# A DLRM tower in blocks of 256 samples with 11 resident tables, instead of blocks of 512 with 9 tables loaded again in each

## The chip, the cores and the metric

One core of one Trainium2 chip. The metric is the device time of one launch in microseconds (us), as the median of several runs.

## What is computed

For each of 2048 samples the kernel fetches one row of 128 floats from each of 26 tables, stacks them behind the sample's dense row (27 features), takes all 351 inner products between two different features, and puts the result through three layers:

```
e = stack([tbl_f[ids[:, f]] for f in range(26)], axis=1)
combined = concatenate([dense[:, None, :], e], axis=1)          # 2048 x 27 x 128
inter = einsum('bfd,bgd->bfg', combined, combined)[:, iu, ju]   # 351 pairs
h = concatenate([dense, inter, dense], axis=1)                  # 2048 x 607
h = maximum(h @ W_top1 + b_top1, 0)                             # 512
h = maximum(h @ W_top2 + b_top2, 0)                             # 256
y = h @ W_top3
```

Twelve tables have 1000 rows, the others 1250, 12500 or 125000. All is in float32. Where the fast float32 matmul (fp32r) is used, an operand is split into a high and a low part, so one product costs two or three matmuls.

## The kernel before

The batch runs in 4 blocks of 512 samples (4 tiles of 128). Three blocks are passes of a loop (`Fori`), the last is written out after it. Inside a block every engine follows two lists made by hand, `BODY` and `TAIL`; in the same lists the tables of the next block are looked up ("ahead").

- **Gathers.** GpSimd (POOL) fetches 17 tables: one indirect DMA (L396) for each table and tile, 128 rows each, 272 in all. TensorE (PE) transposes the rows (`embed`, L416) in groups of 4 features into a PSUM bank, and ScalarE (ACT) copies the bank into `emb` (L535), whose layout is [dimension, sample, feature].
- **Lookups.** 9 tables of 1000 rows are looked up by matmul. For each block and table SyncE (SP) loads the whole table (L331) and the ids, broadcast to 128 partitions (L335). ACT takes the high part (L543), VectorE (DVE) the low part (L640). For each of 8 chunks of 125 rows DVE makes a one-hot of 125x512 (L650), and PE multiplies it with the high and the low part (L436, L438). ACT copies the result into one column of `emb` (L549, L558).
- **Gram.** For each sample PE multiplies `emb[:, s, 1:27]` with `emb[:, s, 0:26]` (L454), four samples side by side in the array; 64 samples fill one bank (128 matmul records, as a float32 matmul leaves two). DVE copies the bank (L663) and transposes 32x32 blocks (L670). ACT, and DVE for the last tile, copy the upper triangle row by row into `pairs` (L565, L677).
- **Layers.** PE transposes `pairs` (`z`, L467), ACT and DVE make high and low parts (L574, L687); layer 1 is 192 and layer 2 is 96 matmuls of 512 columns over all blocks (L485 to L488, L498 to L501). ACT and DVE split the hidden layer (L586, L588, L699). ACT sends y out (L604).

Of the kernel before, what the change touches and what calls it, by code (L numbers as in the profile page):

```python
# [8 lines left out]
FEATURES = TABLES + 1  # L29
# [3 lines left out]
LOOKUPS = 9  # L33
LOOKED_UP = [t for t in range(TABLES) if VOCAB[t] == 1000][:LOOKUPS]
GATHERED = [t for t in range(TABLES) if t not in LOOKED_UP]

ORDER = [0] + [t + 1 for t in GATHERED] + [t + 1 for t in LOOKED_UP]


def pair_rows():  # L40

    rows = []
    for r in range(FEATURES):
        for s in range(r + 1, FEATURES):
            a, b = sorted((ORDER[r], ORDER[s]))
            rows.append(DIM + a * FEATURES - a * (a + 1) // 2 + (b - a - 1))
    return rows


def dlrm_tower(nc, dense, ids_gathered, ids_looked_up, tables, w1_dense, w1_pairs, b1, w2, b2, w3,  # L50
               out):
    fp32, fp32r = mybir.dt.float32, mybir.dt.float32r
    i32, u32 = mybir.dt.int32, mybir.dt.uint32
# [5 lines left out]
    NG = len(GATHERED)  # L59
    ROWED = NG + 1  # L60

    EMBED = [list(range(f, min(f + 4, ROWED))) for f in range(0, ROWED, 4)]
    bank_of = {f: e for e, features in enumerate(EMBED) for f in features}
    CHUNKS = 8
    TROWS = 1000 // CHUNKS
    SIDE = FEATURES - 1
    HALF = 16
    GRAMS = TILE // 4 // HALF * TILES
    KCH = [128, 128, PAIRS - 256, DIM]
    N1, N2 = HIDDEN1 // 128, HIDDEN2 // 128  # L70
    ONE_HOTS = 9
    assert LOOKUPS * CHUNKS % ONE_HOTS == 0

    EARLY = 2
    lookups = [("lookup", i, h) for i in range(LOOKUPS) for h in range(2)]  # L80
    early, halves = lookups[:2 * EARLY], lookups[2 * EARLY:]
    embeds = [("embed", t, e) for t in range(TILES - 2) for e in range(len(EMBED))]

    PARTS = ((3,), (0,), (1, 2))
    LAST = len(PARTS) - 1
    own = [[("layer1", 0, 0)], [("layer1", 1, 0), ("z", 0, 0), ("z", 1, 0), ("z", 2, 0)],
           [("z", 0, 1), ("z", 1, 1)], [("z", 2, 1)],
           [("layer1", 0, 1)], [("layer1", 1, 1)], [("layer1", 0, 2)], [("layer1", 1, 2)],
           [("layer1", 2, p) for p in range(3)], [("layer1", 3, p) for p in range(3)], "E",
           [("layer2", 0)], [("layer2", 1)], "E", [("layer3",)], "E", "E", "E", "E", "E", "E"]  # L90
    TAIL = [("place", i) for i in range(EARLY)] + [("pair", 1)] + halves[:1]
    spaces = own.count("E")
    for k, steps in enumerate(own):
        if steps == "E":
            n = len(embeds) // spaces
            spaces, steps, embeds = spaces - 1, embeds[:n], embeds[n:]
        TAIL += steps

        upto = -(-(k + 1) * len(halves) // len(own))
        if "E" in own[k + 1:k + 2]:  # L100
            upto += upto % 2
        TAIL += [s for s in halves[:upto] if s not in TAIL]
    assert len(TAIL) == len(set(TAIL))
    tile2, tile3 = ([("embed", t, e) for e in range(len(EMBED))] for t in (2, 3))
    BODY = [("gram", 0), ("gram", 1), ("gram", 2), *tile2, ("gram", 3), ("gram", 4),
            *early, *tile3[:-1], ("dense",), ("gram", 5, 0), tile3[-1], ("gram", 5, 1),
            ("split", EARLY + 1), ("pair", 0), ("gram", 6), ("gram", 7)]

# [6 lines left out]
        [("layer2", n) for n in range(N2)] + [("layer3",), ("none",)]  # L115
    assert len(MLP_USES) % 2 == 0
    assert len(EMB_USES) % 3 == 0 and len(MIX_USES) % 3 == 0

    PAIR_TILES = [slice(0, TILES - 1), slice(TILES - 1, TILES)]
# [648 lines left out]
```

## Time and profile before

| | |
|---|---|
| median of 3 runs | 432.58 us (428.92 to 434.95) |
| profiled execution, span from first to last instruction | 432.4 us |
| PE, PEld (weight loads), POOL, DVE, ACT busy | 330.4, 266.8, 308.9, 239.1, 179.4 us |
| granted TensorE clock, mean | 0.881 of 2.4 GHz |

The profiled execution has no other time of its own than its span; it stands 0.2 us under the median. Busy time of an engine is the time in which an instruction of it runs. In the timeline a line is one instruction or several alike; its columns are the start, the length, the engine, the source line and the operation, and in brackets the idle time of the engine before it with what ended it ("issue": nothing that the profile shows). In a line of a group the numbers after the bar are busy time, mean ns of one, and the idle time before.

### The profile page before, as it was taken

What the parts mean: (1) busy time and instruction counts of PE and PEld (TensorE: products, weight loads), DVE (VectorE), ACT (ScalarE), POOL (GpSimd) and SP (SyncE); (2) the same over time, 40 slices, a digit from 0 to 9 for tenths busy, and PEclk for the clock granted to TensorE, in tenths of its full rate; (3) what the DMA queues carried; (4) which work ended last, traced back from release to release, by engine and by line L of the source; (5) the groups of instructions that cost most, each with busy time, mean ns of one, the idle gap of its engine ahead of it and who ended that gap; (6) DMA issues with size and microseconds to landing.
All of it is one profiled execution on the core that took longest, in us unless ns stands there. A gap on an engine that the chain in (4) does not pass through costs nothing.

```text
span 432.4 us, 13310 instructions
## 1 busy us (share of the span) xinstructions
PE 330.4 (76%) x5360; PEld 266.8 (62%) x5360; DVE 239.1 (55%) x471; ACT 179.4 (41%) x363; POOL 308.9 (71%) x280
## 2 busy tenths in 40 slices
PE   0785719677699998286879999376969999867596
PEld 0563517466578876275668877264758887656475
DVE  2776625397569563266768664075666758023531
ACT  2144223720746546220546545420564546323442
POOL 6887878887778877777778878777777877772000
PEclk9899977888979999659969999666879999986699
DMA  5467853435435345426444543526354442221000
GB/s 155 153 177 191 239 167 109 128 92 151 115 110 149 118 122 117 133 52 167 119 130 114 158 116 106 141 55 169 77 172 100 142 123 71 55 57 28 5 0 0
DMA packets 24707, 49.51 MB, mean 115 GB/s; under 512 B 8010, under 2 KB 10586, under 8 KB 24653
## 3 DMA queue, kind: packets, MB, share of 16 engines
q1 hardware_dynamic: 15916, 30.83, 22.4%
q0 software_dynamic: 8704, 17.84, 17.5%
q8 instruction: 47, 0.77, 0.7%
q14 instruction: 8, 0.06, 0.0%
q10 hardware_dynamic: 32, 0.01, 0.0%
HBM read 48.65 MB, written 0.01 MB: 113 GB/s over the span
## 4 chain that ended last, share of the span: by engine, by line
PE 65%; issue 15%; DMA 10%; ACT 5%; DVE 3%; SPq 0%; ACTq 0%; DVEq 0%
PE mix_ps L454 12%; PE emb_ps L436 12%; PE emb_ps L438 11%; PE emb_ps L416 6%; DMA lookup_ids<-ids_looked_up 5%; DMA table<-table 5%; PE mlp_ps L485 4%; PE mlp_ps L488 4%; PE mlp_ps L486 4%; PE mlp_ps L436 3%; PE mlp_ps L438 3%; DVE one_hot L650 2%; ACT emb L535 2%; PE mlp_ps L498 2%; PE mlp_ps L501 2%
## 5 line engine op out<-in xcount | busy, mean ns | idle before, releaser
L396 POOL DMA_INDIRECT rows<-table,gather_ids x272 | 307.9, 1132 | 83.6 <-issue 81.7
L650 DVE TENSOR_SCALAR one_hot<-lookup_ids,row_number 125x512 fp32r<-125x512 int32 x288 | 124.8, 490 | 43.6 <-DMA lookup_ids<-ids_looked_up 17.6
L436 PE MATMUL emb_ps<-one_hot,table_h 125*128 125x512 f32 x224 | 94.2, 421 | 19.1 <-DVE table_l L640 18.7
L454 PE MATMUL mix_ps<-emb 128*26 128x26 f32 x4096 | 57.7, 202 | 54.3 <-issue 51.5
L438 PE MATMUL emb_ps<-one_hot,table_l 125*128 125x512 f32 x224 | 91.9, 410 | 0.0
L454 PEld LDWEIGHTS mix_ps<-emb 128*26 128x26 f32 x4096 | 49.5, 115 | 63.6 <-issue 61.7
L543 ACT ACTIVATE table_h<-table 125x1024 fp32r<-125x1024 f32 x36 | 38.0, 1060 | 88.9 <-DMA table<-table 52.4
L535 ACT ACTIVATE emb<-emb_ps 128x512 f32<-128x512 f32 (+1 forms) x80 | 46.9, 651 | 56.5 <-PE emb_ps L416 53.2
L663 DVE COPY gram<-mix_ps 128x416 f32<-128x416 f32 x32 | 27.8, 874 | 74.3 <-PE mix_ps L454 74.1
L436 PEld LDWEIGHTS emb_ps<-one_hot,table_h 125*128 125x128 f32 x224 | 44.6, 199 | 31.7 <-ACT emb L535 12.1
L549 ACT ACTIVATE emb<-emb_ps 128x512 f32<-128x512 f32 x28 | 34.0, 1215 | 50.2 <-PE emb_ps L438 50.1
L640 DVE TENSOR_TENSOR table_l<-table,table_h 125x1024 fp32r<-125x1024 f32 x36 | 43.6, 1212 | 13.6 <-ACT table_h L543 13.6
L438 PEld LDWEIGHTS emb_ps<-one_hot,table_l 125*128 125x128 f32 x224 | 44.7, 200 | 9.2
L436 PE MATMUL mlp_ps<-one_hot,table_h 125*128 125x512 f32 x64 | 31.0, 484 | 20.2 <-DVE one_hot L650 17.5
L416 PE MATMUL emb_ps<-ident,rows 128*128 128x128 f32 x272 | 42.7, 302 | 1.9 <-ACT emb L549 1.7
L416 PEld LDWEIGHTS emb_ps<-ident,rows 128*128 128x128 f32 x272 | 36.0, 158 | 6.9 <-ACT emb L549 1.9
L436 PEld LDWEIGHTS mlp_ps<-one_hot,table_h 125*128 125x128 f32 x64 | 15.0, 235 | 26.0 <-issue 15.0
L438 PE MATMUL mlp_ps<-one_hot,table_l 125*128 125x512 f32 x64 | 29.8, 466 | 0.0
L565 ACT ACTIVATE pairs<-turned 128x24 f32<-128x24 f32 (+33 forms) x148 | 19.0, 219 | 11.7 <-DVE turned L670 11.7
L699 DVE TENSOR_TENSOR h1l<-h_full,h1h 128x512 fp32r<-128x512 f32 x16 | 11.2, 700 | 22.0 <-ACT h1h L588 22.0
L586 ACT ACTIVATE h_full<-mlp_ps,b_sb 128x512 f32<-128x512 f32 x16 | 11.0, 689 | 20.7 <-PE mlp_ps L488 20.6
L485 PE MATMUL mlp_ps<-zh,w1h 128*128 128x512 f32 (+1 forms) x48 | 19.1, 398 | 0.5 <-ACT zh L574 0.5
(50 smaller groups left out, 278.4 us busy)
## 6 DMA issues: line engine op xcount, KB each, us to landing
table<-table SPq DMA_DIRECT2D x36, 500.0 KB
lookup_ids<-ids_looked_up SPq DMA_DIRECT2D x36, 256.0 KB, 5.4
rows<-table,gather_ids POOLq DMA_INDIRECT x272, 3.9
dense_rows<-dense SPq DMA_DIRECT2D x4, 256.0 KB, 4.1
gram<-w_pairs SPq DMA_DIRECT2D x2, 256.0 KB
gram<-w_dense SPq DMA_DIRECT2D x2, 256.0 KB
h_full<-w SPq DMA_DIRECT2D x1, 512.0 KB
gather_ids<-ids_gathered SPq DMA_DIRECT2D x16, 8.5 KB, 10.2
```

The source lines that it names most:

```text
L396: pool.indirect_dma_start(out=rows[:, t, g, :], out_offset=None, in_=tables[GATHERED[g]], in_offset=bass.IndirectOffsetOnAxis(ap=gather_id ...
L416: last = pe.transpose(bank[:, 128 * k:128 * k + 128], src, ident[:, :])
L436: pe.matmul(bank[:, :], table_h[0:TROWS, i % 2, cols], hot, start=(c == 0), stop=False)
L438: last = pe.matmul(bank[:, :], table_l[0:TROWS, i % 2, cols], hot, start=False, stop=(c == CHUNKS - 1))
L454: last = pe.matmul(bank[32 * j:32 * j + SIDE, SIDE * q:SIDE * q + SIDE], emb[:, s, 1:FEATURES], emb[:, s, 0:SIDE], start=True, stop=True)
L485: pe.matmul(mlp_bank(("layer1", n))[:, :], w1h[0:k, c, cols], high, start=(c == 3), stop=False)
L535: act.activation(emb[:, t * TILE:(t + 1) * TILE, EMBED[e][0]:EMBED[e][0] + k], emb_bank(("embed", t, e))[:, 0:128 * k].rearrange("p (k s) ...
L543: act.activation(table_h[0:TROWS, i % 2, :], table[0:TROWS, i % 2, :], ACT.Copy) \
L549: act.activation(emb[:, :, ROWED + i], emb_bank(("lookup", i, 1))[:, :], ACT.Copy) \
L640: dve.tensor_tensor(table_l[0:TROWS, i % 2, :], table[0:TROWS, i % 2, :], table_h[0:TROWS, i % 2, :].bitcast(fp32), ALU.subtract) \
L650: dve.tensor_scalar(one_hot[0:TROWS, hot_slot(i, c), :], lookup_ids[0:TROWS, i % 2, :], row_number[0:TROWS, c:c + 1], None, ALU.is_equal) \
L663: dve.tensor_copy(gram[:, :, HALF * n:HALF * n + HALF].rearrange("p r q -> p q r"), mix_bank(("gram", n))[:, 0:SIDE * HALF].rearrange("p ( ...
```

## The change

The kernel is written anew around one list, `STEPS`: each step gets a time in units of a block (`at(time, ...)`), the list is sorted by it, and each engine runs its part of the list, written out without a loop.

- 8 blocks of 256 samples, that is 16 tiles of 128.
- 11 tables are loaded once. Their high and low parts stay in SBUF (`table_hl`). `raw`, where they land, has 6 slots and lies on the half of `emb` that block 1 uses first. In block 0 only 6 of them are looked up, from block 1 on all 11: 83 lookups. The first lookup of block 1 waits for all 11 low parts.
- Tiles 0 and 1 gather 20 tables, the other 14 tiles gather 15: 250 gathers. The rows lie in a ring of 7 groups; a gather waits until PE has transposed the group 7 before. The dense row is the last feature of a tile's last group.
- A one-hot is 128x256 from 16-bit ids; the ring holds 8. A chunk is 128 rows (tables are padded to 1024). Two tables share a PSUM bank and are copied together.
- A gram bank (64 samples) is filled in one run (`BURSTS = 1`). ACT copies it instead of DVE. A tile's triangle is copied by 10 ACT instructions, in bands of 5 rows.
- Layer matmuls have 256 columns; there are 384 and 192 of them. ACT writes the hidden layer's full value back into its PSUM bank, and DVE subtracts from there.
- The build takes `dynamic_dma_scratch_size=4096`.

The core of the diff:

```diff
-    TILE, TILES = 128, 4
-    BLOCK = TILE * TILES
+    TILE = 128
+    TILES = BATCH // TILE
     BLOCKS = BATCH // BLOCK
+    GROUP = [grouped(list(range(FIRST_LOOKUPS if t < BLOCK // TILE else LOOKUPS, FEATURES))) for t in range(TILES)]
+    ROW_SLOTS = 7
+    HALF, BURSTS = 16, 1
+    HOTS = 8
+    RAW, LIDS = 6, 4
+    LOOKS = [(b, i) for b in range(BLOCKS) for i in range(LOOKUPS if b else FIRST_LOOKUPS)]
+    def look_time(k, h):
+        b, i = LOOKS[k]
+        return b - 1 + (i + h / 2) / (LOOKUPS if b else FIRST_LOOKUPS) + (0.02 if b else 0.0)
+    def embed_time(t, e):
+        return (t / 2 - 0.7 if t >= 3 else (-0.2, 0.25, 0.56)[t]) + 0.06 * e * 4 / len(GROUP[t])
+    for i in range(LOOKUPS):
+        at(-1.6 + 0.1 * i if i >= RAW else -2.0 + i / 100, "load", i)
+        at((-1.5, -1.3)[i] if i < 2 else -1.1 + 0.1 * i, "split", i)
+    for k in range(len(LOOKS)):
+        at(look_time(k - LIDS, 1) + 0.002 if k >= LIDS else -1.995 + k / 100, "lids", k)
+        for h in range(2):
+            at(look_time(k - 1, h) + 0.001 if k >= 1 else -1.4 + h / 50, "hots", k, h)
+            at(look_time(k, h), "look", k, h)
...
+                at(t / 2 + 0.05 + 0.24 * (n % 2) + 0.06 * h + (0.07 if t == 1 else 0.0), "gram", n, h)
+        at(t / 2 + 0.54, "pairs", t)
...
+        for c in range(2):
+            at(u + 1.06 + 0.02 * c, "z", u, c)
+        for n in range(N1):
+            at(u + 1.13 + 0.09 * n, "l1", u, n)
+        for n in range(N2):
+            at(u + 1.54 + 0.09 * n, "l2", u, n)
+        at(u + 1.74, "l3", u)
...
             def hots(k, h):
...
+                    wait(dve, hot_used, n - HOTS + 1)
+                    dve.tensor_scalar(hot[:, n % HOTS, :], lids[:, k % LIDS, :],
+                                      row_number[:, c:c + 1], None, ALU.is_equal).then_inc(hot_ready, 1)
...
             def look(k, h):
...
+                    if k < FIRST_LOOKUPS:
+                        pe.wait_ge(table_low, k + 1)
+                    elif k == FIRST_LOOKUPS:
+                        pe.wait_ge(table_low, LOOKUPS)
...
+                for e, group in enumerate(GROUP[t]):
+                    use = GROUP_NO[t, e]
+                    wait(pool, embeds_done, use - ROW_SLOTS + 1)
...
-    nc = bacc.Bacc("TRN2", target_bir_lowering=False, num_devices=1)
+    nc = bacc.Bacc("TRN2", target_bir_lowering=False, num_devices=1, dynamic_dma_scratch_size=4096)
```

## Rows read from the trace of the kernel before

**Rows 1.** The page: busy tenths, and the granted clock, in 40 slices of 10.8 us.

```profile
PE   0785719677699998286879999376969999867596
...
PEclk9899977888979999659969999666879999986699
```

**Rows 2.** Groups of instructions by line: the gathers.

```profile
L396 POOL DMA_INDIRECT rows<-table,gather_ids x272 | 307.9, 1132 | 83.6 <-issue 81.7
```

**Rows 3.** Timeline of all engines: the last gather, and the last row transposes.

```profile
392.28 0.94 POOL L396 DMA_INDIRECT rows<-table,gather_ids  x1 [0.30 <-issue]
...
397.76 0.44 PE L416 MATMUL emb_ps<-ident,rows 128*128 128x128 f32 x2
```

**Rows 4.** All gathers of line 396: first and last start, and the time to landing.

```profile
L396 POOL DMA_INDIRECT rows<-table,gather_ids x272: 940/947/3814, 2.7 to 392.3; - x136
...
DMA to landing us min/median/max: 2.4/3.9/8.0
```

**Rows 5.** Timeline of PE: gram runs, at the low clock, then at the high one.

```profile
179.76 2.03 PE L454 MATMUL mix_ps<-emb 128*26 128x26 f32 x127 [2.48 <-issue]
183.79 1.97 PE L454 MATMUL mix_ps<-emb 128*26 128x26 f32 x127 [2.00 <-issue]
...
399.08 1.28 PE L454 MATMUL mix_ps<-emb 128*26 128x26 f32 x128 [0.42 <-issue]
402.90 1.28 PE L454 MATMUL mix_ps<-emb 128*26 128x26 f32 x128 [2.55 <-issue]
```

**Rows 6.** Who waited for whom: PE in the gram.

```profile
PE mix_ps L454 <- issue: 51.5, 26, 3.9
```

**Rows 7.** Timeline of PE: 512-column steps, low clock, after a wait, 72 at the high clock.

```profile
12.84 0.63 PE L436 MATMUL mlp_ps<-one_hot,table_h 125*128 125x512 f32 x1
13.27 0.63 PE L438 MATMUL mlp_ps<-one_hot,table_l 125*128 125x512 f32 x1
...
17.34 0.50 PE L436 MATMUL mlp_ps<-one_hot,table_h 125*128 125x512 f32 x1 [1.91 <-DVE one_hot L650]
...
129.02 0.40 PE L436 MATMUL emb_ps<-one_hot,table_h 125*128 125x512 f32 x1
...
145.80 0.39 PE L436 MATMUL emb_ps<-one_hot,table_h 125*128 125x512 f32 x1
```

**Rows 8.** Timeline of PE: row transposes, at the high clock and at the low one.

```profile
170.44 1.04 PE L416 MATMUL emb_ps<-ident,rows 128*128 128x128 f32 x8
189.45 3.56 PE L416 MATMUL emb_ps<-ident,rows 128*128 128x128 f32 x17
```

**Rows 9.** Timeline of DVE and POOL in two bursts of DVE.

```profile
16.80 4.84 DVE L650 TENSOR_SCALAR one_hot<-lookup_ids,row_number 125x512 fp32r<-125x512 int32 x12
...
18.10 1.28 POOL L396 DMA_INDIRECT rows<-table,gather_ids  x1 [0.30 <-issue]
19.68 2.07 POOL L396 DMA_INDIRECT rows<-table,gather_ids  x1 [0.30 <-issue]
22.06 0.94 POOL L396 DMA_INDIRECT rows<-table,gather_ids  x1 [0.30 <-issue]
```

**Rows 10.** Groups by line, of DVE and ACT.

```profile
L650 DVE TENSOR_SCALAR one_hot<-lookup_ids,row_number 125x512 fp32r<-125x512 int32 x288 | 124.8, 490 | 43.6 <-DMA lookup_ids<-ids_looked_up 17.6
...
L543 ACT ACTIVATE table_h<-table 125x1024 fp32r<-125x1024 f32 x36 | 38.0, 1060 | 88.9 <-DMA table<-table 52.4
...
L549 ACT ACTIVATE emb<-emb_ps 128x512 f32<-128x512 f32 x28 | 34.0, 1215 | 50.2 <-PE emb_ps L438 50.1
L640 DVE TENSOR_TENSOR table_l<-table,table_h 125x1024 fp32r<-125x1024 f32 x36 | 43.6, 1212 | 13.6 <-ACT table_h L543 13.6
```

**Rows 11.** Windows of one block each: busy time by engine, clock, DMA share.

```profile
172.00:272.00 100.00, 80.79 (x1346) 66.08 (x1346) 58.17 (x116) 44.55 (x93) 78.59 (x71) 0.88 0.45 124
```

**Rows 12.** Windows of 4 us at the start, the same columns, GB/s last.

```profile
7.00:11.00 4.00, 0.00 (x0) 0.00 (x0) 0.92 (x1) 1.06 (x1) 3.08 (x4) 1.00 0.76 221
44.00:48.00 4.00, 4.00 (x20) 3.20 (x19) 1.58 (x5) 0.83 (x1) 3.08 (x4) 1.00 1.05 306
```

More of the change, by code:

```diff
@@ L40, in pair_rows @@
 def pair_rows():
     rows = []
[L43 to L46, printed above, removed]
-    return rows
-def dlrm_tower(nc, dense, ids_gathered, ids_looked_up, tables, w1_dense, w1_pairs, b1, w2, b2, w3,
-               out):
+    for r, s in pair_list():
+        a, b = sorted((ORDER[r], ORDER[s + 1]))
+        rows.append(DIM + a * FEATURES - a * (a + 1) // 2 + (b - a - 1))
@@ L104, in dlrm_tower @@
[L104 to L107, printed above, removed]
-    EMB_USES = [s for s in TAIL + BODY if s[0] == "embed" or (s in halves and s[2] == 1)]
-    MIX_USES = [("gram", n) for n in range(GRAMS)] + [("z", 0), ("z", 1), ("z", 2)] + [("none",)]
@@ new lines, in dlrm_tower, with pair_of_looks @@
+    for j in range(6):
+        at(0.05 + 0.13 * j, "weights", j)
+    for u in range(BLOCKS):
+        late = u == BLOCKS - 1
+        for c in range(2):
[5 more added lines that the diff above has]
+        at(u + 1.74, "l3", u)
+    STEPS = [step for _, _, step in sorted(timed)]
+    def pair_of_looks(k):
+        first = k - LOOKS[k][1] % 2
+        return first, min(first + 1, k - LOOKS[k][1] + len([1 for b, _ in LOOKS if b == LOOKS[k][0]]) - 1)
@@ L378, in _ @@
+            sp.dma_start(gather_ids[:, 0, :], ids_gathered[:, 0, :]).then_inc(first_ids_in, 16)
+            run({"load": load, "lids": load_lids, "drow": drow, "weights": weights})
         @block.gpsimd
@@ L440, in lookup @@
-                    last.then_inc(hot_used, 1)
-            def grams(b, n, part=None):
-                if n % 2 == 0:
-                    need = [u for u in EMB_USES if u[0] == "lookup" or u[1] == n // 2]
-                    pe.wait_ge(emb_copied, emb_no(b, need[-1]) + 1)
-                if part != 1:
-                    pe.wait_ge(*mix_before(b, ("gram", n)))
-                bank = mix_bank(("gram", n))
-                for q in (range(HALF) if part is None else range(HALF)[part * HALF // 2:][:HALF // 2]):
+                    pe.matmul(bank, table_hl[:, i, 0, cols], hot[:, n % HOTS, :], start=(c == 0), stop=False)
@@ new lines, in look, with embed @@
+                    pe.matmul(bank, table_hl[:, i, 1, cols], hot[:, n % HOTS, :],
+                              start=False, stop=(c == CHUNKS - 1)).then_inc(hot_used, 1)
+            def embed(t, e):
+                use, n = ("embed", t, e), GROUP_NO[t, e]
+                pe.wait_ge(rows_in[n % ROW_SLOTS], rows_landed(n))
+                if e == len(GROUP[t]) - 1:
+                    pe.wait_ge(dense_in[t % 2], 16 * (t // 2 + 1))
+                wait_emb_bank(pe, use)
+                for q in range(len(GROUP[t][e])):
+                    last = pe.transpose(emb_bank(use)[:, 128 * q:128 * q + 128], rows[:, n % ROW_SLOTS, q, :], ident[:, :])
+                last.then_inc(embeds_done, 1)
@@ new lines, in gram @@
+            def gram(n, h):
+                t, side = n // 2, n % 2
+                bank = mix_ps[n % 2]
+                if h == 0:
+                    if side == 0:
+                        b = t // 2
+                        pe.wait_ge(emb_placed, max(
+                            [placed["look", pair_of_looks(k)[1], 1] for k in range(len(LOOKS)) if LOOKS[k][0] == b] +
+                            [placed["embed", t, e] for e in range(len(GROUP[t]))]))
+                    wait(pe, gram_out, n - 1)
+                for q in range(h * HALF // BURSTS, (h + 1) * HALF // BURSTS):
```

836 lines of the change are left out of this document (369 added, 467 removed).

## The prediction

> **What bounds the kernel now.** I read the page first, then the groups by line, the waits, and the timeline of each engine. PE is busy nearly throughout, and in every block there are some slices at five or six tenths in which the clock falls as well [rows 1]. But busy shares don't name the bound. POOL issues 272 gathers; behind each it idles 0.30 us, put down to "issue", so it waits for nobody [rows 2], and it goes on from 2.7 to 393.2 us [rows 3, 4]. That is 390.5 / 272 = 1.436 us a gather. The last rows land some 4 us later, and PE's last two row transposes start at 397.76, as soon as they can [rows 3, 4]. From there to the end (432.4) it is 34.7 us of layers. So the gathers set the end, with that tail behind them.
>
> PE is bound just as tightly. Its steps at the high clock (2.4 GHz): a 512-column matmul 0.232 us (190 steps between lines such as 133.95 and 134.19), at the low clock (1.2 GHz) 0.427 [rows 7]; a row transpose (1.04 - 0.3) / 7 = 0.106 us, at the low clock 0.204 [rows 8]; a gram bank 1.28 us, at the low clock 2.03 [rows 5]. Before: 864 x 0.232 + 336 transposes x 0.106 + 32 banks x 1.28 = 200 + 36 + 41 = 277 us at the high clock, some 2 us of layer 3 with it 279. The rest up to 432 is 51.5 us of idle "issue" in the gram [rows 6], the start, the tail, and the low clock, which holds (1 - 0.881) x 2 = 24% of the time. After each 128 records of gram PE stands still for 2 to 2.5 us, so that a bank takes about 4 us whatever the clock [rows 5]. 128 matmuls and their 128 weight loads are 256 instructions, 16 KB.
>
> The page of the Trainium skill on Runtime: NRT & Kernel Launch (Instruction fetch mechanics) says that instructions come in blocks of 16 KiB, 256 of them, and that a taken branch breaks the prefetch. The gaps of 2.0 us after 127 or 128 records [rows 5] agree with the block size. By that rule a run of 64 samples amid slower work finds its block there.
>
> **The change, POOL.** 250 gathers instead of 272. Undisturbed one takes 0.94 + 0.30 = 1.25 us [rows 3, 4]: 250 x 1.25 = 312.5. What lies above that is DVE: during 12 one-hots in a row (4.84 us) gathers took 1.28 and 2.07 us, behind it 0.94 again [rows 9]. All stalls before: 307.9 - 272 x 0.944 = 51 us [rows 2, 4], on 288 one-hots 0.18 us each [rows 10]. After there are 83 x 8 = 664 one-hots, but of 256 columns: one of 512 steps every 4.84 / 12 = 0.40 us [rows 9]; taken as 0.13 fixed + 0.27 for the columns, half of it is 0.26, and all are 664 x 0.26 = 173 us against 115. Bounds: nothing (0), and 664 x 0.18 = 120 us if each one costs as much as now. Between them: a gather waits for the rest of the DVE instruction that runs, which goes with count x length squared: 664 x 0.26^2 / (288 x 0.40^2) = 0.97, so 50 us; with burst time (1.85 against 1.25 us a gather in the burst [rows 9]) it is a third of 173 = 58. I take 55, near both. POOL ends at 2.7 + 312.5 + 55 = 370, the last rows land at 374.
>
> The Trainium skill, SBUF — State Buffer (Who interferes with whom), has it that a DVE instruction in a two-port mode locks GpSimd out for its whole length. [rows 9] agree. By a strict lock with no gap between one-hots the stall would go with their whole time, 173 us instead of 55; the two gathers that got through within the 4.84 us speak against that.
>
> The ring of 7 groups lets POOL be 23 gathers ahead at the start. Gather 24 needs the first embed group, which PE does behind its fifth lookup, at about 30 us; POOL is there at 2.7 + 23 x 1.47 = 37. It costs nothing; if lookups start 10 us late it costs 3. The smaller descriptor memory: issue to landing is 3.9 us [rows 4], so 3 to 4 gathers are under way. I take 0 for it, and its upper end is a rival.
>
> **PE.** Lookups are 83 x 16 = 1328 matmuls of 256 columns, layers 576. No row shows 256 columns. Below: 256 / 2.4 = 0.107. Above: the first matmul after a wait took 0.50 instead of 0.39 to 0.40 us [rows 7], so a weight load that nothing hides costs 0.11, and 0.107 + 0.11 = 0.217. The nearest row is the transpose, which loads 128 columns of weights each and still steps by 0.106 [rows 8]; so the load hides behind 0.107. 512 columns step by 0.232, 0.019 over 512 / 2.4; kept whole it gives 0.126, halved 0.116. I take 0.126. Sum: 1904 x 0.126 = 240, (266 + 48) transposes x 0.106 = 33, 32 banks x 1.28 = 41, layer 3 1: 315 us against 279. PE thus gets 36 us more work; what it should get back is the 51.5 us in the gram, since a gram bank is now followed by 20 to 50 slower instructions at a time. I leave 10 us of gaps in the whole (a third of the banks run out of instructions for 1 us).
>
> **The start.** Before, only two tables were under way, and one was loaded each 6 to 9 us. Now six go out at once: 3.0 MB at 221 GB/s [rows 12] is 14 us, and the memory queues have given 306. DVE then is the slowest: up to the first lookup of block 1 it has 52 one-hots x 0.26 and 11 low parts x 1.21 [rows 10] = 27 us behind about 11, so 38 us. PE would be quick enough, but tile 3's rows, gather 70, come at 2.7 + 70 x 1.47 (the pace of the DVE-laden start) + 3.9 = 109.5. PE waits for them, since embed stands in its list before the lookups of block 2. Behind them PE has 1632 matmuls x 0.126 = 206, 240 transposes 25, 28 banks 36, 1: 268 us, plus 10 of gaps, plus 16 idle in the tail: 404 at the high clock throughout. With a tenth of the time at the low clock it is 268 / 0.95 = 282, so 418. POOL's path and PE's path are again nearly even.
>
> **The tail.** Behind the last embed stand four gram banks (5), 12 transposes (1), 144 layer matmuls x 0.126 (18), layer 3 (0.3): 25 us. The chain of the last bank waits for ACT's copy (1.0), DVE's transposes (1.05), the triangle (10 x 0.22), high and low parts before layer 1 (1.4), before layer 2 (1.4), and the output (3), and block 6 has two such waits of 1.5: with the hand-overs 16 us. So 41, with 0.5 for the embed and 1.5 for the low clock 43.
>
> **Sum.** 2.7 + 312.5 + 55 + 3.9 + 43 = 417.1 us, against 432.4 of the profiled span, which is the median of the runs shown (432.58) within 0.2. All other edits lie beside this: 25 splits of tables fewer on ACT and DVE (25 x 1.06 and 25 x 1.21 us [rows 10]); the gram copies on ACT (32 x 1.0); ACT comes to some 205 us and DVE to 235 of 417. If that cover went, each late step of ACT would cost PE its 1 us, some 14 times. DMA moves about 29 MB instead of 49.5 and is at 45% of its time now [rows 11].
>
> **Rivals.**
> 1. Slower: one-hots cost POOL by their count, 0.18 us each, 120 us. For it: the first burst [rows 9], where gathers took up to 2.07 us. Against: shorter instructions leave sooner. 2.7 + 312.5 + 120 + 47 = 482 us. It decides from (432.4 - 2.7 - 312.5 - 47) / 664 = 0.106 us a one-hot.
> 2. The 256-column step isn't half: each 10 ns over 0.126 costs 16 us on PE's path; from 0.141 the kernel is no faster, at 0.217 it takes 404 + 1632 x 0.091 = 553. Against: the transposes [rows 8].
> 3. PE's clock and small waits: at the low clock for 24% of the time as now, 268 / 0.88 = 305, so 441 us. For it: PE waits for rows in every tile, as POOL is even with it. Against: the slices at the low clock now stand at the gram's gaps [rows 1, 5], which go.
> 4. Better: short one-hots let the gathers through (25 us of stalls), a step of 0.116, 5 us of gaps: POOL's path 2.7 + 312.5 + 25 + 47 = 387, PE's 404 - 16 - 5 + 7 for the clock = 390, and some waits, 395 us.
> 5. The change doesn't do what it says: the smaller descriptor memory lets one gather go at a time, 250 x 3.9 = 975 us. Against: nothing in the trace shows that it is full.
>
> **How the numbers follow.** The forecast has 38%, rival 4 22%, rival 3 17%, rival 1 and what lies between it and the forecast 13%, rival 2 7%, rival 5 3%. Predicted: 417 us. The range, 392 to 450, takes in rival 4, rival 3 and the lower part of rival 1. A measurement of this kernel tells 2% (424 to 441 is no change). Faster: rival 4 and the forecast whole, 60%; same: rival 3 and the mild cases of 1 and 2, 22%; slower: the rest of 1, 2, 3 and 5, 18%.
>
> **What would show it.** Gathers that end near 370 with a mean of about 1.47 us from start to start; the 256-column step at 0.126; gram banks of 1.3 us without a gap of 2 us behind most of them; PE waiting for rows up to about 110 us; a tail of 43 us behind the last landing; a mean clock over 0.92. The prediction is wrong if POOL ends before 340 or after 400, if the step is over 0.14, or if PE never waits for rows and yet ends late.

## The result, and the profile after

| | before | after |
|---|---|---|
| median (runs) | 433.68 us (428.92 to 434.95, 4) | 397.9 us (397.15 to 398.95, 4) |
| span of the profiled execution | 432.4 us | 395.9 us |
| mean granted clock | 0.881 | 0.966 |

The ratio is 0.920, 95% interval 0.914 to 0.926: 8% faster, where 3.6% (417 us) was forecast. It stands inside the range, near the time of rival 4.

The page of the changed kernel: busy time by engine, and busy tenths with the granted clock in 40 slices of 9.9 us.

```profile
PE 344.4 (87%) x6378; PEld 323.1 (82%) x6378; DVE 261.1 (66%) x765; ACT 183.2 (46%) x443; POOL 239.5 (61%) x258
...
PE   1777499458999999999999999999999899998556
...
POOL 6777777777777777777777676757674752000000
PEclk9989889988999999999999999999999989999969
```

The dips of PE and of the clock in every block [rows 1] are gone: from slice 11 to 36 PE is at 80% or more and the clock nearly full. Groups by line, gathers, one-hots and gram, against [rows 2, 10] (after the bar: busy us, mean ns, idle before):

```profile
L340 POOL DMA_INDIRECT rows<-table,gather_ids x250 | 238.6, 954 | 91.5 <-issue 73.5
L571 DVE TENSOR_SCALAR hot<-lids,row_number 128x256 fp32r<-128x256 int16 x664 | 206.1, 377 | 27.7 <-PE emb_ps L368 24.9
...
L394 PE MATMUL mix_ps<-emb 128*26 128x26 f32 x4096 | 53.0, 193 | 6.9 <-issue 3.4
```

All gathers of the changed kernel (min/median/max ns, first and last start), with POOL's idle time, against [rows 4]:

```profile
L340 POOL DMA_INDIRECT rows<-table,gather_ids x250: 940/944/1802, 2.7 to 330.7; - x125
its engine sat idle before it (us, times) until:
  issue: 73.5, 241
  PE emb_ps L378: 17.0, 8
```

A gather takes 954 ns on average instead of 1132: next to nothing holds it up. POOL even waits 17.0 us for PE (the ring is full), and is through at 331.6, 64 us ahead of the end. PE's waits (us in total, times, longest):

```profile
PE emb_ps L367 <- DVE hot L571: 19.6, 9, 8.0
PE emb_ps L378 <- DMA rows<-table,gather_ids: 10.6, 5, 3.4
PE mix_ps L394 <- issue: 3.4, 2, 1.9
```

The 51.5 us of "issue" in the gram [rows 6] have come down to 3.4. This list leaves out idle times of less than 0.15 us, and there are such pauses: most gram banks take about 1.8 us or more. One of the middle, and one of those later on (timeline of PE):

```profile
207.52 1.82 PE L394 MATMUL mix_ps<-emb 128*26 128x26 f32 x128
302.67 1.27 PE L394 MATMUL mix_ps<-emb 128*26 128x26 f32 x128
```

From the start of the first matmul of a bank to the start of what follows it, 23 of the first 25 banks take 1.7 us or more, and the six from 325 us to 368 us take 1.2 to 1.3. In the bank at 207.52 two matmuls start 0.22 and 0.27 us behind the one before them, which the bank at 302.67 doesn't have; the weight loads in it wait 0.18 us for "issue". What these pauses are is not shown.

The chain of work that ended last, by engine, and the timeline where it passes from POOL to PE:

```profile
PE 68%; POOL 16%; issue 8%; ACT 3%; DVE 2%; DMA 1%
```

```profile
87.01 0.95 POOL L340 DMA_INDIRECT rows<-table,gather_ids  x1 [0.30 <-issue]
...
90.49 1.11 PE L378 MATMUL emb_ps<-ident,rows 128*128 128x128 f32 x4 [3.39 <-DMA rows<-table,gather_ids]
...
94.35 0.60 PE L378 MATMUL emb_ps<-ident,rows 128*128 128x128 f32 x4
```

Those at 90.49 are the third of tile 3's four groups. Its last gather, the 70th, starts at 90.76, and its last group is transposed at 94.35 without a wait. By the chain the gathers set the pace up to 90.5 us, from there PE alone. Three windows, split at 90.5 and behind the last row transposes (us, then busy and count of PE, PEld, DVE, ACT, POOL, the clock, the DMA share, GB/s):

```profile
0.00:90.50 90.50, 57.92 (x835) 51.63 (x835) 63.95 (x162) 37.13 (x61) 67.99 (x77) 0.92 0.52 155
90.50:354.20 263.70, 257.97 (x4859) 245.59 (x4860) 189.33 (x588) 127.03 (x320) 171.54 (x181) 0.99 0.28 66
354.20:395.90 41.70, 28.46 (x688) 25.85 (x685) 7.81 (x15) 19.04 (x63) 0.00 (x0) 0.92 0.01 2
```

In the middle PE is busy 98% of the time at 0.99 of full clock.

### The profile page after: what moved, and what is told of

The parts are those of the page before. It is cut to its first block, busy times and chain, and to the rows that moved or that the text cites. A ratio compares the mean times of both kernels' runs of the same rounds, so it can differ in the third digit from the quotient of the medians.

```text
span 395.9 us, 14710 instructions
## 1 busy us (share of the span) xinstructions
PE 344.4 (87%) x6378; PEld 323.1 (82%) x6378; DVE 261.1 (66%) x765; ACT 183.2 (46%) x443; POOL 239.5 (61%) x258
## 4 chain that ended last, share of the span: by engine, by line
PE 68%; POOL 16%; issue 8%; ACT 3%; DVE 2%; DMA 1%
PE emb_ps L367 17%; POOL rows L340 16%; PE emb_ps L368 16%; PE mix_ps L394 11%; PE emb_ps L378 6%; PE mlp_ps L425 4%; PE mlp_ps L427 4%; PE mlp_ps L426 4%; PE mlp_ps L436 2%; PE mlp_ps L438 2%; PE mlp_ps L437 2%; ACT gram_sb L491 1%; PE mlp_ps L447 1%; DVE hot L571 1%; PE mlp_ps L407 1%
## 5 line engine op out<-in xcount | busy, mean ns | idle before, releaser
L340 POOL DMA_INDIRECT rows<-table,gather_ids x250 | 238.6, 954 | 91.5 <-issue 73.5
L571 DVE TENSOR_SCALAR hot<-lids,row_number 128x256 fp32r<-128x256 int16 x664 | 206.1, 377 | 27.7 <-PE emb_ps L368 24.9
L367 PE MATMUL emb_ps<-hot,table_hl 128*128 128x256 f32 x664 | 183.8, 309 | 21.2 <-DVE hot L571 19.6
L368 PE MATMUL emb_ps<-hot,table_hl 128*128 128x256 f32 x664 | 172.6, 291 | 0.0
L367 PEld LDWEIGHTS emb_ps<-hot,table_hl 128*128 128x128 f32 x664 | 132.0, 199 | 27.5 <-DVE hot L571 10.3
L368 PEld LDWEIGHTS emb_ps<-hot,table_hl 128*128 128x128 f32 x664 | 132.9, 200 | 0.0
L464 ACT ACTIVATE emb<-emb_ps 128x512 f32<-128x512 f32 (+1 forms) x113 | 79.0, 721 | 58.5 <-PE emb_ps L368 30.4
L394 PEld LDWEIGHTS mix_ps<-emb 128*26 128x26 f32 x4096 | 44.1, 104 | 16.7 <-issue 9.6
L491 ACT ACTIVATE gram_sb<-mix_ps 128x416 f32<-128x416 f32 x32 | 29.6, 925 | 56.8 <-PE mix_ps L394 56.8
L378 PE MATMUL emb_ps<-ident,rows 128*128 128x128 f32 x266 | 40.7, 276 | 11.0 <-DMA rows<-table,gather_ids 10.6
L588 DVE STREAM_TRANSPOSE turned<-gram_sb 128x832 uint32<-128x832 uint32 x16 | 16.7, 1045 | 37.0 <-ACT gram_sb L491 37.0
L425 PE MATMUL mlp_ps<-zh,w1h 128*128 128x256 f32 (+1 forms) x96 | 28.1, 292 | 2.7 <-DVE zl L593 2.7
L426 PE MATMUL mlp_ps<-zh,w1l 128*128 128x256 f32 (+1 forms) x96 | 27.3, 285 | 0.0
L427 PE MATMUL mlp_ps<-zl,w1h 128*128 128x256 f32 (+1 forms) x96 | 27.2, 284 | 0.0
L425 PEld LDWEIGHTS mlp_ps<-zh,w1h 128*128 128x128 f32 (+1 forms) x96 | 18.6, 194 | 3.8 <-DVE zl L593 3.8
```

The lines of the kernel that those rows point to most:

```text
L340: pool.indirect_dma_start(out=rows[:, use % ROW_SLOTS, q, :], out_offset=None, in_=tables[GATHERED[g]], in_offset=bass.IndirectOffsetOnAxi ...
L367: pe.matmul(bank, table_hl[:, i, 0, cols], hot[:, n % HOTS, :], start=(c == 0), stop=False)
L368: pe.matmul(bank, table_hl[:, i, 1, cols], hot[:, n % HOTS, :], start=False, stop=(c == CHUNKS - 1)).then_inc(hot_used, 1)
L378: last = pe.transpose(emb_bank(use)[:, 128 * q:128 * q + 128], rows[:, n % ROW_SLOTS, q, :], ident[:, :])
L394: last = pe.matmul(bank[32 * j:32 * j + SIDE, SIDE * q:SIDE * q + SIDE], emb[:, s, 1:FEATURES], emb[:, s, 0:SIDE], start=True, stop=True)
L425: pe.matmul(bank, w1h[0:k, c, cols], high, start=(c == 3), stop=False)
```

## The experiments

"Stalls" below are what the gathers take above 0.945 us each, summed over those longer by more than 0.05: 50.8 us before, 2.4 after. They are read from one profile of each kernel. The same kernel profiled twice gave 2.4 and 1.9 us, and the one with ten tables 3.7 and 4.4, but experiment 3 shows that two profiles can differ by 5. My theory at first was that 16-bit ids, or the low parts that are no longer made in every block, let the gathers through; the rival was the shorter one-hots.

The first two groups of runs were made on two chips on which the kernel before takes about 700 us, the later ones on chips where it takes 431 to 433, as in the first comparison. Each ratio is with the kernel before on the same chip. The expectations for the first group were written for a chip of 433 us, so their absolute times can't be held against it.

**1. Ten tables, 16-bit and 32-bit ids, and the kernel before with 16-bit ids.**

```diff
-FIRST_LOOKUPS, LOOKUPS = 6, 11
+FIRST_LOOKUPS, LOOKUPS = 6, 10
```

> The changed kernel with 10 resident tables instead of 11, so that one table moves from lookups to gathers: 7 x 16 = 112 matmuls of 256 columns fewer (112 x 0.12 = 13.4 us), 14 transposes (1.5 us) and 14 gathers (17.5 us of POOL) more. Theory 'PE is the bound since the gathers are no longer held up': about 386 us, the last gather near 345 us. Rival 'the gathers still set the end': 398 + 10 to 17 us, so 408 to 415.

The same with 32-bit ids:

```diff
-        lids = sb("lids", [128, LIDS, BLOCK], i16)
+        lids = sb("lids", [128, LIDS, BLOCK], i32)
```

> The kernel with 10 resident tables, the ids of the one-hots in 32 bits instead of 16, all else alike. Theory 'the 16-bit source takes the one-hot out of the mode that holds up POOL': a one-hot steps by 0.26 us instead of 0.30, a gather's mean goes from 0.95 us to 1.10 or more, POOL ends some 40 us later, the kernel takes 400 to 430 us. Rival 'it is their length: 256 columns let gathers through': gathers stay at 0.95 to 1.0 us and the time within 3 us of the run with 16 bits.

The kernel before with 16-bit ids:

```diff
-        lookup_ids = sb("lookup_ids", [128, 2, BLOCK], i32)
+        lookup_ids = sb("lookup_ids", [128, 2, BLOCK], mybir.dt.int16)
```

> The kernel before, with the ids of its 512-column one-hots in 16 bits instead of 32. Theory '16-bit source': the gather's mean falls from 1.13 to 0.95 us and the last one ends near 345 us instead of 393; a one-hot steps by 0.57 to 0.60 us instead of 0.40. PE is bound as tightly, and DVE gets 50 us more, so 420 to 440 us. Rival 'length': gathers stay at 1.13 us, since the columns are still 512.

Measured: 605.2 us (ratio 0.865, 0.863 to 0.868), 605.3 us (0.866, 0.862 to 0.871) and 707.3 us (1.000, 0.993 to 1.007), with the kernel before at 701.6. Stalls 3.7, 5.1 and 13.8 us; a one-hot took 362 and 363 ns in the first two. For one-hots of 256 columns the type of the ids changes nothing, so that part of my theory falls. For those of 512 columns the time is the same too; no profile of the unchanged kernel was taken on such a chip, so there the stalls have no base. These chips show what else can bind. PE's gram group of the kernel before with 16-bit ids:

```profile
L454 PE MATMUL mix_ps<-emb 128*26 128x26 f32 x4096 | 99.0, 205 | 289.7 <-issue 287.3 <-ACT emb L535 2.2
```

and a piece of its timeline of PE in a gram:

```profile
177.04 0.20 PE L454 MATMUL mix_ps<-emb 128*26 128x26 f32 x1 [1.15 <-issue]
178.44 0.28 PE L454 MATMUL mix_ps<-emb 128*26 128x26 f32 x2 [1.20 <-issue]
179.16 0.20 PE L454 MATMUL mix_ps<-emb 128*26 128x26 f32 x1 [0.44 <-issue]
181.27 0.26 PE L454 MATMUL mix_ps<-emb 128*26 128x26 f32 x2 [1.90 <-issue]
```

PE gets one or two matmuls and then stands for 0.4 to 1.9 us: 287 us in all, against 51.5 [rows 6]. The profile calls this "issue", a wait for nothing that it shows; that PE waits for its instructions is my reading. POOL in turn waits 196 us for PE with ten tables. Since everything else is stretched by it, stalls on these chips compare only with each other.

**2. The gram banks filled in four bursts**, as a slow supply of instructions would suggest, on either kind of chip.

```diff
-    HALF, BURSTS = 16, 1
+    HALF, BURSTS = 16, 4
```

> The changed kernel with a gram bank filled in 4 bursts of 16 samples between other steps instead of in one run of 64. Theory 'a burst of 256 instructions outruns the instruction fetch': the idle 'issue' in front of and in the gram (some 10 us) goes, 390 to 395 us. Rival 'each change between gram and other matmuls costs PE 0.1 to 0.2 us': 96 more changes, 405 to 415 us.

> Gram banks in 4 bursts of 16 samples, beside one run on the same chip. On a chip with little 'issue' idle: 0 to 8 us less if the fetch still costs what little is left, 5 to 15 us more if each change of kind costs PE 0.1 to 0.2 us. On a chip with much of it: less time than one run, since 64 instructions outrun the fetch less than 256 do (the run with bursts on the first such chip took 594 us, 10 tables 605).

Measured: on the first kind 593.9 us, ratio 0.848 (0.842 to 0.855). Eleven tables in one run were not measured there; ten in one run gave 0.865. On the other 403.0 us, 0.932 (0.922 to 0.942), against 397.7 us, 0.920 (0.911 to 0.930), for the changed kernel in the same group. PE's waits there:

```profile
PE mlp_ps L407 <- ACT pairs L509: 12.7, 8, 3.4
...
PE mix_ps L394 <- issue: 1.9, 1, 1.9
```

In the profile of the changed kernel of this group the same two waits are 4.0 and 6.1 us. Added up from the start of one record to the start of the next, without idle times above 0.15 us, the gram takes 45.1 us in bursts and 54.2 in one run. So the bursts do take out some 13 us of pauses in the gram. They lose more than that elsewhere. PE waits 8.7 us longer for the triangle, as a bank is full later, and all matmuls other than gram and transposes take 272.7 us instead of 263.2: 49 more of them stand first behind gram or transposes, where one steps by 0.21 us instead of 0.12. Both theories of the expectation were half right, and together they come to 5 us more.

**3. What holds a gather: added DVE work of one and of two inputs.** To the kernel with ten tables, run again, 22 instructions of 1024 columns were added on DVE, once a subtraction of two SBUF operands, once a copy; nothing reads their result.

> The changed kernel with 10 resident tables once more, on whatever chip it gets; on the first one every kernel, that of before too, took some 60% longer, with PE idle for 'issue'. On a chip on which the kernel of before takes about 433 us: 386 us by 'PE is the bound', 408 to 415 us by 'the gathers still set the end'. Gathers 0.95 us each either way.

```diff
+                    dve.tensor_tensor(spare[:, :], table_hl[:, 0, 0, :].bitcast(fp32), table_hl[:, 0, 1, :].bitcast(fp32), ALU.subtract)
```

> The kernel with 10 tables plus 22 DVE subtractions of 128x1024 with both inputs in SBUF (1.21 us each), in front of one-hots of every third lookup; their result is used by nothing. Theory 'it is the low part of the tables, with two inputs in SBUF, together with the one-hots that follow at once, that holds up the gathers': 0.9 to 1.3 us of gather stall for each, 20 to 28 us in all against 3. Rival 'one-hots of 512 columns did it by themselves, of 256 they don't': stall stays under 8 us. The time rises by less than 10 us in both cases, POOL having slack.

```diff
+                    dve.tensor_copy(spare[:, :], table_hl[:, 0, 0, :].bitcast(fp32))
```

> The same with 22 DVE copies of 128x1024, one input in SBUF, instead of the subtractions (about 0.7 us each). Theory 'any long DVE instruction on two SBUF ports holds gathers up for its length': 0.4 to 0.7 us each, 9 to 15 us in all. Rival 'only two inputs do': under 4 us.

Measured: stalls 4.4, 9.9 and 10.4 us; times 608.2, 604.7 and 604.0 us, with no difference worth reading. The totals mislead: 3.8 and 6.0 us of them (0.9 in the run without additions) fall in the first 46 us, and the first added instruction runs behind 106 us, so those can't come from the additions. Beside the subtractions (1220 ns each) run 20 gathers, of which 11 are held up, by 4.0 us in all; beside the copies (689 ns each) 11, of which 10 are, by 2.5 us. That is 0.18 us for a subtraction and 0.11 for a copy, and for each microsecond that DVE spends on them about the same (0.15 and 0.17). Both kinds hold gathers up, and far less than the 0.9 to 1.3 and 0.4 to 0.7 us that the theories had; in size it is nearer to the rivals, but that only two inputs do it is not so. Some of these gathers also ran beside one-hots, so the shares are upper ones. The Trainium skill, SBUF — State Buffer (Who interferes with whom), has a one-input instruction in a two-port mode lock GpSimd out, and a two-input one contend with its reads only; that both hold gathers up here agrees with the first, and of the second it shows that gathers are among what is held.

**4. The low parts of the tables made short in the kernel before**: 32 of 1024 columns, the rest zero. This leaves out most of the low parts' contribution to the lookups.

```diff
-                dve.tensor_tensor(table_l[0:TROWS, i % 2, :], table[0:TROWS, i % 2, :],
-                                  table_h[0:TROWS, i % 2, :].bitcast(fp32), ALU.subtract) \
+                dve.tensor_tensor(table_l[0:TROWS, i % 2, 0:32], table[0:TROWS, i % 2, 0:32],
+                                  table_h[0:TROWS, i % 2, 0:32].bitcast(fp32), ALU.subtract) \
```

> The kernel before, with the low part of a looked-up table taken for 32 of 1024 columns only (the rest is left at zero), so that this DVE instruction takes about 0.1 to 0.2 us instead of 1.21; one-hots and matmuls as before. Theory 'low parts with one-hots behind them make the stalls': gather stalls fall from 51 to 10 to 20 us, the last gather ends near 355 to 365 us instead of 393, the kernel takes 415 to 430 us, since PE is bound as tightly. Rival 'the 288 one-hots of 512 columns make them': stalls stay over 40 us and the time within 1%.

> The kernel before with the low part for 32 of 1024 columns. On a chip with 433 us for the kernel before: gather stalls 6 to 15 us instead of 51, the last gather ends near 355 us; the time 415 to 430 us if PE is bound as tightly, under 400 us if the gathers alone had set the end.

Measured on the first kind of chip: 713.6 us, 1.011 (1.004 to 1.019), stalls 6.4 us. On the other: 429.9 us, ratio 0.996 (0.992 to 1.000). Its gathers:

```profile
L396 POOL DMA_INDIRECT rows<-table,gather_ids x272: 940/944/3767, 2.7 to 366.3; - x136
```

Stalls fell from 50.8 to 24.7 us, not to the 6 to 15 that I expected, and the last gather starts 26.0 us earlier than in [rows 4], not near 355. The kernel gains 0.4%, with an interval that reaches to no gain. In this profile (of the fastest of its ten runs, 425.3 us) the last two row transposes start at 388.8, 22.5 us behind the start of the last gather, where it was 5.5 before. So the gathers did not set the end of the kernel before.

**5. The changed kernel again, and with ten tables**, on a chip of the common kind. The edit is that of experiment 1.

> The changed kernel as it is, as the base for the runs beside it, since the two chips so far took 700 us for the kernel before. On a chip like that of the first measurement: 0.92 of before, 398 us. On one like the last two, on which PE idles 250 to 300 us for 'issue' in the gram: 600 to 620 us, about 0.87, since 10 tables gave 0.865 and gram runs are of the same 256 instructions.

> 10 resident tables, beside 11 on the same chip. Theory 'PE is the bound, 112 matmuls of 0.12 us fewer': 10 to 13 us less than with 11. Rival 'the gathers set the end': 10 to 17 us more.

Measured: 397.7 us (0.920) and 389.1 us, ratio 0.899 (0.890 to 0.909). Ten tables need 14 gathers more and 56 one-hots, 112 matmuls fewer. POOL still ends at 334.8 (last start 333.8), the mean gather is 953 ns, and the time falls by 8.6 us. 112 x 0.12 = 13.4 us less on PE, and 1.4 more for 14 transposes, make 12; 10 to 13 were expected, and 8.6 came. PE waits 12.5 us for rows instead of 9.1 now, which is what is missing. PE is the bound of the changed kernel behind its start, and POOL has room there.

**6. DVE's instructions cut to 256 columns in the kernel before.** Every one-hot of 512 columns by two instructions, then every low part by four, then both; all else stays.

```diff
+                    for p in range(2):
+                        part = slice(p * BLOCK // 2, (p + 1) * BLOCK // 2)
-                    dve.tensor_scalar(one_hot[0:TROWS, hot_slot(i, c), :], lookup_ids[0:TROWS, i % 2, :],
+                        made = dve.tensor_scalar(one_hot[0:TROWS, hot_slot(i, c), part],
+                                                 lookup_ids[0:TROWS, i % 2, part],
```

> The kernel before, with every one-hot of 512 columns made by two DVE instructions of 256 columns (576 instead of 288); PE, ACT and all transfers unchanged. Length theory (a gather is held up for the rest of the DVE instruction that runs, so short ones hardly hurt): the gathers that only one-hots overlap lose under 3 us instead of about 10 to 20, all stalls together fall from 51 to about 30 us, the gather's mean from 1.13 to about 1.06 us. Count theory (each one-hot costs 0.18 us or more whatever its length): stalls rise, to 70 us or more. Bandwidth theory (what counts is DVE's busy time): stalls rise with it, to about 60 us. Time: DVE's busy time grows by about 25 us beside slack, so within 2 per cent of before by all three, and at most 1 per cent less by the length theory.

```diff
+                for p in range(4):
+                    part = slice(256 * p, 256 * p + 256)
-                dve.tensor_tensor(table_l[0:TROWS, i % 2, :], table[0:TROWS, i % 2, :],
+                    made = dve.tensor_tensor(table_l[0:TROWS, i % 2, part], table[0:TROWS, i % 2, part],
```

> The kernel before, with the low part of each table made by four DVE instructions of 256 columns instead of one of 1024 (144 instead of 36), the same columns in all. Length theory: the part of the stalls that goes with the low parts (26 us by the run with 32 columns) goes nearly whole, 25 to 30 us of stalls are left. Theory that two-input instructions hold up gathers whatever their length: stalls stay near 50 us. Time within 1 per cent of before in both.

> The kernel before with both edits: one-hots in halves of 256 columns and low parts in quarters of 256 columns. Length theory: stalls of under 10 us, the gather's mean under 0.98 us, last gather start near 355 us or earlier, and yet a time within 2 per cent of before, as PE bounds it too (424 to 434 us). Rival (something other in the changed kernel, such as 128 partitions, 16-bit ids or fewer one-hots side by side, lets its gathers through): stalls of 40 us or more.

Measured, with the stalls sorted by the DVE instructions that run during the gather (us, and the number of gathers; a few small classes are left out):

| | before | one-hots halved | low parts quartered | both |
|---|---|---|---|---|
| ratio | 1 | 1.009 (1.004 to 1.014) | 0.999 (0.994 to 1.003) | 1.018 (1.008 to 1.028) |
| all stalls | 50.8 | 27.3 | 44.2 | 25.1 |
| beside one-hots alone | 9.8 (40) | 0.2 (2) | 10.6 (46) | 0.1 (1) |
| one-hots and a low part | 21.6 (35) | 10.8 (18) | 19.8 (32) | 3.3 (18) |
| those and a low part of the hidden layer | 11.3 (5) | 11.6 (4) | 5.7 (3) | 16.7 (3) |

Twice as many one-hots of half the length, 181 us of DVE's time instead of 125, hold up almost nothing: 9.8 us become 0.2. The count theory and the one that goes by DVE's busy time both fall, and "something else in the changed kernel" isn't needed, since only the length (and with it the count) was changed here. For the low parts the length matters little as long as long one-hots stand behind them (19.8 against 21.6), and much when those are short as well (3.3 against 10.8). So the length theory missed for them alone: it had 25 to 30 us left with the low parts quartered, and 44.2 were.

I had expected under 10 us with both cut, a last gather near 355 and 424 to 434 us. It was 25.1 us, 375.3 and 439.6 us. Two thirds of what is left (16.7 us) sit in three gathers. The timeline of DVE and POOL around the longest:

```profile
240.32 1.42 DVE L642 TENSOR_TENSOR table_l<-table,table_h 125x256 fp32r<-125x256 f32 x4
241.05 10.36 POOL L396 DMA_INDIRECT rows<-table,gather_ids  x1 [0.30 <-issue]
...
241.66 2.18 DVE L654 TENSOR_SCALAR one_hot<-lookup_ids,row_number 125x256 fp32r<-125x256 int32 x8
...
243.76 0.68 DVE L704 TENSOR_TENSOR h1l<-h_full,h1h 128x512 fp32r<-128x512 f32 x1
244.36 2.18 DVE L654 TENSOR_SCALAR one_hot<-lookup_ids,row_number 125x256 fp32r<-125x256 int32 x8
...
246.46 1.42 DVE L642 TENSOR_TENSOR table_l<-table,table_h 125x256 fp32r<-125x256 f32 x4
...
247.80 0.68 DVE L704 TENSOR_TENSOR h1l<-h_full,h1h 128x512 fp32r<-128x512 f32 x1
248.41 2.19 DVE L654 TENSOR_SCALAR one_hot<-lookup_ids,row_number 125x256 fp32r<-125x256 int32 x8
```

From 240.3 to 250.6 DVE has no gap, and the gather that began meanwhile ends at 251.4, 0.8 us behind it. Two more ended so, 0.8 us behind the last DVE instruction of an unbroken run: one of 6.9 us in this kernel and one of 6.9 us in that with halved one-hots. So a gather can stay out until DVE pauses, short instructions or not. It isn't the rule: of the gathers that began and ended inside an unbroken run of this kernel, 28 of 178 took over 1.0 us, and none over 2.7. What makes the difference is open. The Trainium skill, same page and section, says of DVE in a two-port mode that whoever issues first gets the shared ports for the whole of its instruction; the trace agrees in that a gather stands while DVE keeps its pace, but here the gather stayed out for a whole run of instructions.

The last gather of this kernel starts at 375.3 instead of 392.3, and its last row transposes run like this (timeline of PE):

```profile
399.81 3.41 PE L416 MATMUL emb_ps<-ident,rows 128*128 128x128 f32 x15
404.04 0.69 PE L416 MATMUL emb_ps<-ident,rows 128*128 128x128 f32 x2
```

The last two start 29 us behind the start of the last gather, 6 us later than before [rows 3], and the kernel is 1.8% slower (with 56 us more work on DVE for the halved one-hots, which may be why; no run tells). Once more: earlier gathers are worth nothing there.

**7. Ten tables, eight of them looked up in the first block.**

```diff
-FIRST_LOOKUPS, LOOKUPS = 6, 11
+FIRST_LOOKUPS, LOOKUPS = 8, 10
```

> The changed kernel with 10 resident tables and 8 of them looked up in the first block. Against the run with 10 tables and 6 in the first (389.1 us, 0.899 of before) 4 gathers fewer ahead of tile 3's rows, 5 us, and 2 lookups more on PE, 32 x 0.12 = 3.8 us. If the early gathers bound the start up to tile 3's rows: 384 to 387 us, 0.89 of before. If PE's sum alone counts: 393 us, 0.908.

Measured: 384.0 us, ratio 0.891 (0.884 to 0.898), the fastest version here. The run with six in the first block (389.1 us, 0.899, 0.890 to 0.909) was made on another chip and the two intervals overlap, so the difference of 5 us between the two is likely, not certain. PE's row transposes of the early tiles that waited for rows (timeline of PE):

```profile
84.15 1.11 PE L378 MATMUL emb_ps<-ident,rows 128*128 128x128 f32 x4 [0.51 <-DMA rows<-table,gather_ids]
89.28 0.90 PE L378 MATMUL emb_ps<-ident,rows 128*128 128x128 f32 x3 [2.31 <-DMA rows<-table,gather_ids]
```

PE waits 4.3 us for rows where it waited 12.5 with six in the first block. PE's waits for rows fell by 8.2 us and those for one-hots rose by 4.5, against 3.8 us more work; the granted clock was higher too (0.963 against 0.943 in the profiles), and how much of the gain that is isn't shown. Until about 90 us the gathers are the bound, as forecast, and it pays to move work from them to PE there, and the other way round behind it.

## Why the prediction came out as it did

**What bounds the kernel before.** "So the gathers set the end" was wrong. I took it from the order of the last gather and the last transposes [rows 3, 4], which are 5.5 us apart, while a gather lands after 3.9. What I should have asked is whether PE waited for rows. PE's longest waits in the trace of before, in their order:

```profile
PE emb_ps L436 <- DVE table_l L640: 18.7, 5, 9.2
PE mlp_ps L436 <- DVE one_hot L650: 17.5, 4, 11.8
PE emb_ps L416 <- ACT emb L549: 4.3, 8, 0.7
```

Together with the gram's "issue" [rows 6] these are all above 3 us, and none is for rows of a gather. The two runs in which the last gather starts 17 and 26 us earlier confirm it: +1.8% and -0.4%; the second is the clean one. PE "just as tightly" was the true half of the sentence. What the kernel gained, it gained on PE: idle time fell from 102 to 51.5 us and the low clock from 24% of the time to 7%. The loop that went with the change isn't the reason for the gaps in the gram: the last block of the kernel before, written out behind the loop, has 11.8 us of them, the blocks in it 9.8, 14.8 and 15.0. No run takes the gaps away alone.

**The failed step: 55 us of stalls.** They measured 2.4. I mixed count times length squared with the burst time, and both take each one-hot's share as smooth; in fact halving the length ends the stall beside one-hots altogether (0.2 us in 576, 0.7 in 664 of the changed kernel). Also I charged all 51 us of before to one-hots, though 26 of them go when the low parts are short. With 2.4 in place of 55 POOL ends, by the same sum, at 2.7 + 312.5 + 2.4 = 318; it ended at 332, since the ring made it wait 17 us. The bound at which I called the prediction wrong, POOL done before 340, was passed. The whole sum with 2.4 would give 364.5 us, and the kernel took 395.9: POOL's path, which the sum goes by, no longer sets the end. A smaller slip: three gathers lie within the burst of [rows 9], not two, the first of them 1.29 us long; the mean of 1.85 us had it in.

**PE's path** then decides. Forecast: tile 3's last rows at 109.5 and from there 308 us to the end, a tenth of the time at the low clock. Measured: 94.35, when PE transposes them, and 301.5. The 15 us at the start follow from the same wrong stalls, 70 x (1.47 - 1.25) = 15.4, and they are the larger part of the difference between 417 and 395.9, since the two paths had come out even (417 and 418).

The 6.5 us behind it hide errors that cancel; that this part came out near is in part luck. Added up from start to start, with the idle times above 0.15 us apart (the measured terms hold the low clock):

| behind tile 3's last rows, us | forecast | measured |
|---|---|---|
| 1632 matmuls of 256 columns | 206 | 211.2 |
| transposes | 25 | 23.4 |
| 28 gram banks, and their gaps | 36 + 10 | 46.6 + 3.4 |
| layer 3 | 1 | 3.9 |
| other idle time, and the output | 16 | 13.1 |
| low clock | 14 | in the above |

So most of what the full clock gave back was spent on gram banks of 1.66 us instead of 1.28, and on the matmuls.

**The sizes of its terms.** A piece of PE's timeline in the lookups:

```profile
198.46 0.28 PE L367 MATMUL emb_ps<-hot,table_hl 128*128 128x256 f32 x1
198.58 0.28 PE L368 MATMUL emb_ps<-hot,table_hl 128*128 128x256 f32 x1
198.70 0.28 PE L367 MATMUL emb_ps<-hot,table_hl 128*128 128x256 f32 x1
198.82 0.28 PE L368 MATMUL emb_ps<-hot,table_hl 128*128 128x256 f32 x1
...
199.42 0.60 PE L378 MATMUL emb_ps<-ident,rows 128*128 128x128 f32 x4
199.77 0.36 PE L367 MATMUL emb_ps<-hot,table_hl 128*128 128x256 f32 x1
199.98 0.28 PE L368 MATMUL emb_ps<-hot,table_hl 128*128 128x256 f32 x1
```

- The 256-column step is 0.12 us, between the two estimates of 0.116 and 0.126; the weight load hides behind it, as read from the transposes. But the first one behind transposes or gram steps by 0.21 (from 199.77 to 199.98), which the forecast had at nothing; 82 of the 1632 are such, and with the low clock in it the mean is 0.129. So the 10 us that the shorter step should have brought went elsewhere.
- Transposes (0.60 - 0.3) / 3 = 0.10 us: right. A gram bank at 1.28 us holds only for the seven that ran without a pause; the mean of the 28 is 1.66, 10.8 us more in all.
- Gaps in the gram: 10 us forecast; PE idles 3.4 us for "issue" there in long gaps, and 10.8 us are in the short pauses inside the banks, so 14. Most of the 51.5 us came back, as forecast. That it is because slower instructions stand between the banks fits, and is not shown.
- Clock: 0.966 measured, "over 0.92" forecast. Rival 3, the clock low for 24% of the time, fell: with the long gaps gone PE waits mostly early and in the tail, and there the clock is at 0.92 and 0.92; in the middle it is at 0.99.
- The start: DVE was the slowest, busy 33.8 of the first 40 us, and PE waited 19.6 us for one-hots and later 10.6 us for rows. Right in kind.
- The tail: 41.7 us from the last row transposes on, forecast 43. But the forecast meant it behind the last landing, and the rows had lain ready: POOL was done 22 us before PE took them. Timeline of PE at its beginning:

```profile
354.87 1.27 PE L394 MATMUL mix_ps<-emb 128*26 128x26 f32 x128 [0.33 <-ACT emb L464]
356.71 0.87 PE L407 MATMUL mlp_ps<-ident,pairs 128*128 128x128 f32 x6 [0.58 <-ACT pairs L509]
...
358.77 0.38 PE L425 MATMUL mlp_ps<-zh,w1h 128*128 128x256 f32 x1 [0.84 <-DVE zl L593]
```

**The rivals.** Rival 1 (482 us) rested on the count of one-hots; the halved one-hots refute it. Rival 2 fell with the step of 0.12. Rival 5 fell too: no gather waits for another, 241 of them start 0.30 us behind the one before. Rival 4 gave 395 us against 395.9, and was right in kind: the gathers get through, the step is shorter, PE's path decides. That it hit within 1 us is luck: it had 25 us of stalls for 2.4, a step of 0.116 for a mean of 0.129, 5 us of gaps for 14, and tile 3's rows still at 109.5 for 94.35. I gave it 22% against 38% for the forecast; the main reason to prefer the forecast was the stall estimate.

## What to carry to other kernels

Before an engine is named the bound because its work ends late, ask of the engine behind it whether it ever waits for it: the list of PE's waits had no row for gathered rows, and that was worth more than the closeness of two times. Where a cost by contention isn't shown for the new size of instruction, neither count nor busy time scales it; give both sides their chance, and sum every path with both values before one is chosen. When two resources are balanced stage by stage, the balance can be tuned by one number per stage: here 8 tables looked up in the first block and 10 later, instead of 6 and 11, gave another 3% (0.891 against 0.920). And a list of waits that leaves out idle times below some length can miss a cost that is paid in small coin: here some 11 us, in pauses inside 28 gram banks, show only when the time from start to start is added up.

## What the runs showed of the hardware that I had not expected

- In bursts of eight beside gathers, a one-hot of 256 columns takes DVE 0.31 us (31 bursts of the changed kernel); in its three bursts without a gather, 0.27, and in the three within the gather of 10.4 us also 0.27. So DVE, too, pays for the meeting: some 0.04 us a one-hot. At 512 columns (the kernel before, bursts of four) it is 0.42 to 0.43, beside gathers that are held up and beside those that aren't.
- One gather stood still for 10.4 us in an unbroken run of short DVE instructions, while 137 of the 163 that began and ended in such runs of over 3 us took less than 1.0.
- The same kernel took 431 to 433 us on some chips and 702 to 708 on others. The difference shows as PE's "issue" in the gram: 287 us in the version with 16-bit ids, which takes the same time there, against 51.5, while a gram matmul takes 205 ns against 202. Variants of the change help there more (ratio 0.865 with ten tables, 0.848 with eleven and the bank in four bursts); the change itself wasn't run there. What PE waits for on these chips isn't shown.
